# Normalising attention's output straight from PSUM with centred weights, a sort spread over more steps, and later scatters, in an eight-image convolution, scan, attention and expert kernel

## The reference, cut to what matters

```
x = x + ss2d(group_norm(x))      # depthwise conv, scan over 2304 tokens, 256 x 16 states
t = t + attention(ln(t))
t = t + moe(ln(t))               # 8 experts, each token goes to 2 of them

def attention(x):                # linear attention, 8 heads of 16
    q, k, v = split(layer_norm(x, norm_gamma) @ w_qkv.T)
    q = softmax(q, -1) * scale
    k = softmax(k, -2)           # over the tokens
    out = (q @ (k.T @ v)) @ w_out.T
    return (out - mean(out)) * rsqrt(var(out) + 1e-5) * out_gamma
```

## Time and profile before

| | |
|---|---|
| median of three runs | 3913.13 us (3910.83 to 3918.53) |
| the profiled execution: time, span | 3908.72 us, 3906.9 us |
| scans, first to last start | 88 to 3415 us |
| busy: PE, DVE, ACT, POOL | 81%, 76%, 65%, 74% of the span |
| weight loads of PE (beside its matmuls) | 52% |

### The profile page before, as it was taken

One profiled execution on the slowest core, in us unless ns is written; L12 is line 12 of the kernel. 1 busy time (PEld: TensorE's weight loads), 2 busy tenths in 40 slices (PEclk: granted clock), 3 DMA queues, 4 the chain that ended last, 5 costly groups with the idle time before them and its releaser, 6 DMA issues.

```text
span 3906.9 us, 68984 instructions
## 1 busy us (share of the span) xinstructions
PE 3163.4 (81%) x17390; PEld 2012.8 (52%) x17390; DVE 2983.4 (76%) x5234; ACT 2553.7 (65%) x6158; POOL 2909.4 (74%) x3055
## 2 busy tenths in 40 slices
...
GB/s 89 221 146 129 157 124 162 120 161 137 221 177 263 153 211 197 222 221 163 233 178 244 158 208 194 231 212 162 231 185 260 157 202 195 235 150 182 241 233 109
...
## 3 DMA queue, kind: packets, MB, share of 16 engines
...
HBM read 596.93 MB, written 100.07 MB: 178 GB/s over the span
## 4 chain that ended last, share of the span: by engine, by line
PE 24%; POOL 22%; issue 21%; DVE 15%; ACT 11%; DMA 4%; ACTq 2%; SPq 1%; POOLq 1%; DVEq 0%; PEldq 0%
POOL prod L698 10%; DVE state L1582 6%; PE ps_conv L901 5%; PE ps_main L967 4%; DVE ps_x L1569 3%; POOL got L821 3%; PE ps_g L1085 2%; DMA dt_rep<-dt_dram 2%; POOL rows_in L798 2%; PE ps_g L1092 2%; POOL hidden L810 2%; PE ps_y L981 2%; ACT dt_rep L1206 2%; PE ps_h L1073 2%; PE ps_x L915 1%
## 5 line engine op out<-in xcount | busy, mean ns | idle before, releaser
L698 POOL TENSOR_TENSOR prod<-state,c_rep 128x384 f32<-128x384 f32 x1536 | 1532.7, 1007 | 608.5 <-DVE state L1582 588.7
L1582 DVE TENSOR_TENSOR_SCAN state<-dt_rep,carry,ps_x 128x384 f32<-128x384 f32 x1280 | 1285.8, 1005 | 0.0
L1569 DVE TENSOR_TENSOR ps_x<-ps_x,db_rep 128x384 f32<-128x384 f32 x1536 | 852.9, 555 | 243.0 <-PE ps_x L915 223.7
L1206 ACT ACTIVATE dt_rep<-dt_rep,vecs 128x384 f32<-128x384 f32 x1536 | 917.8, 615 | 137.9 <-DMA dt_rep<-dt_dram 77.7
L915 PE MATMUL ps_x<-x_stack,copy 96*128 96x384 bf16 x1536 | 534.2, 350 | 310.8 <-DVE state L1582 306.4
L901 PE MATMUL ps_conv<-gx,w_conv 128*128 128x384 f32 x1728 | 689.6, 507 | 8.0 <-DVE parts L1599 4.6
L915 PEld LDWEIGHTS ps_x<-x_stack,copy 96*128 96x128 bf16 x1536 | 153.9, 100 | 681.6 <-DVE state L1582 493.1
L1390 ACT ACTIVATE g_sb<-ps_g,w_down 128x128 f32<-128x128 f32 x1032 | 304.2, 371 | 231.1 <-PE ps_g L1092 226.3
L901 PEld LDWEIGHTS ps_conv<-gx,w_conv 128*128 128x128 f32 x1728 | 301.1, 195 | 216.6 <-issue 129.6
L1073 PE MATMUL ps_h<-u_t,w_up 128*128 128x128 f32 x2064 | 327.5, 298 | 104.0 <-DVE silu L1799 80.0
L810 POOL TENSOR_TENSOR hidden<-g_sb,silu 128x384 f32<-128x384 f32 x344 | 343.7, 999 | 83.9 <-ACT u_out L1396 74.8
(11 more groups left out here) (256 smaller groups left out, 4958.7 us busy)
## 6 DMA issues: line engine op xcount, KB each, us to landing
dt_rep<-dt_dram SPq DMA_DIRECT2D x384, 768.0 KB
...
dt_dram<-dt SPq DMA_DIRECT2D x192, 96.0 KB
...
```

The costliest lines, as they stand in the source:

```text
L698: pool.tensor_tensor(prod[:, k % HS, :], state[:, k % HS, :], c_rep[:, c % 2, :], ALU.mult).then_inc(s_prod.sem, 1)
L1206: act.activation(dt_rep[:, g % XS, q, :], dt_rep[:, g % XS, q, :], ACT.Exp, scale=decay_rate).then_inc(s_decay.sem, 1)
L1569: dve.tensor_tensor(x_n, x_n, db_rep[:, c % 2, :], ALU.mult).then_inc(s_inflow.sem, 1)
L1582: dve.tensor_tensor_scan(state[:, k % HS, :], dt_rep[:, g % XS, q, :], ps_x[k % XB][:, 0:T], init, ALU.mult, ALU.add).then_inc(s_state.sem, 1)
```

## The change

The output of attention is no longer evacuated, normalised, scaled and added in passes of their own. At the start the weights `w_proj` are centred (their mean over the output channels is taken off, so that the product's mean is zero), and a second copy is multiplied by `out_gamma`. One matmul of 256 columns for a block then gives both the centred output and the scaled one. ACT squares the first half out of PSUM with a running sum, takes logarithm and exponential for 1/rms, and DVE adds the second half times this to `acc`, straight from PSUM. This goes by pairs of blocks (`ap0` to `ap8`, at steps T_AP), with `qT` set between them at T_QT. `acc` now lies in `u_tok`, t1 is read a second time at step 66, and the first read goes to `k_tok`. The sort's steps are spread over 134 to 164, some of its instructions are fused; the first scatter moves from 146 to 168, the second half from 183 to 208 (step 16 of the next pass). Expert tiles, gathers, top-2 and transposes move by some steps.

```diff
-T_XLOAD = 114
+T_XLOAD = 112
-SEQ2 = ("qT0", "qT1", "ao0", "qT2", "ao1", "qT3", "ao2", "qT4", "ao3", "qT5", "ao4", "ao5")
-T_SEQ2 = 68
-T_AGAIN, T_STAT2, T_NORM2, T_STAT3 = 81, 82, 86, 98
-T_GAMMA = tuple(87 + g + g // 2 for g in range(NC))
-T_NORM3 = (102, 103, 105, 107, 110, 112)
-T_UT, T_LOGIT = (105, 105, 110, 110, 115, 117), (115, 122)
-T_TOP = ((119, 0, 9), (126, 9, 14), (127, 14, 18))
-T_PLACE = ((120, 0, 3), (121, 3, 6), (122, 6, 9), (128, 9, 12), (129, 12, 15), (130, 15, 18))
-T_CHOSEN, T_RANK, T_SORT = 132, 135, 136
+T_QT, T_AP = (64, 66, 67, 71, 75, 79), (68, 69, 72, 73, 76, 77, 80, 81, 83)
+NA = NT // 2
+T_AGAIN, T_STAT2 = 66, 88
+T_ACC = (79, 87)
+T_NORM2 = (92, 94, 97, 100, 103, 106)
+T_UT, T_LOGIT = (96, 98, 104, 105, 110, 112), (110, 119)
+T_TOP = ((115, 0, 9), (123, 9, 14), (124, 14, 18))
+T_PLACE = ((116, 0, 3), (117, 3, 6), (118, 6, 9), (125, 9, 12), (126, 12, 15), (127, 15, 18))
+T_CHOSEN, T_RANK = (134, 136), 140
+T_SORT = (143, 146, 149, 152, 154, 156, 158, 161, 164)
-AMONG = (81, 84, 87, 90, 93, 96, 99, 102, 107, 112, 119, 126, 132)
+AMONG = (88, 91, 93, 95, 98, 100, 103, 106, 109, 114, 118, 125, 131)
-T_GATHER = tuple(2 * SC + t for t in (34, 36, 39, 41, 44, 46, 49, 51, 66, 69, 72, 75, 102, 105, 108, 111, 114, 117))
+T_GATHER = tuple(2 * SC + t for t in (34, 36, 39, 41, 44, 46, 49, 51, 66, 69, 72, 75, 86, 90, 94, 98, 102, 106))
-T_SCATTER = tuple(146 + 15 * k // 8 for k in range(NT)) + tuple(183 + 15 * k // 8 for k in range(NT))
-T_SCATTER_LAST = tuple(146 + k for k in range(NT)) + tuple(165 + k for k in range(NT))
-T_HOLD, SOONEST = T_GATHER[0] - 1, 264
-ENDED, SPREAD, RESUMED = 34, T_SCATTER_LAST[0], T_SCATTER_LAST[-1] + 8
+T_SCATTER = tuple(168 + 2 * k for k in range(NT)) + tuple(208 + 15 * k // 8 for k in range(NT))
+T_SCATTER_LAST = tuple(T_SCATTER[0] + k for k in range(NT)) + tuple(T_SCATTER[0] + 19 + k for k in range(NT))
+ENDED, SPREAD, RESUMED = 50, T_SCATTER_LAST[0], T_SCATTER_LAST[-1] + 8
+T_HOLD, SOONEST = T_GATHER[0] - 1, T_W + SC - (RESUMED - 3)
...
-        acc = x_in = q_tok
+        acc, x_in = u_tok, q_tok
...
# POOL
-                    if t == T_GAMMA[g]:
-                        due(pool, s_xn, m, NC + g + 1)
-                        pool.tensor_tensor(k_tok[:, tiles, :], k_tok[:, tiles, :],
-                                           out_gamma[:, :].unsqueeze(1).broadcast_to([P, TT, D]), ALU.mult).then_inc(s_gam.sem, 1)
-                    if t == T_GAMMA[g] + 1:
-                        pool.tensor_tensor(acc[:, tiles, :], acc[:, tiles, :], k_tok[:, tiles, :], ALU.add).then_inc(s_acc.sem, 1)
...
# PE
-                elif kind == "ao":
-                    for k in range(TT):
-                        ins = pe.matmul(o[:, P * k:P * k + P], turned[:, T * g + P * k:T * g + P * k + P], ctx_o[:, :],
-                                        start=True, stop=True)
+                elif kind == "ap":
+                    for k in range(2):
+                        r = P * (2 * g + k)
+                        ins = pe.matmul(o[:, 2 * D * k:2 * D * k + 2 * D], turned[:, r:r + P], ctx_o[:, :], start=True, stop=True)
...
# ACT, one step behind PE
+                elif kind == "ap":
+                    logs()
+                    act.wait_ge(*full(m, name))
+                    tiles = slice(2 * g, 2 * g + 2)
+                    for k in range(2):
+                        t = 2 * g + k
+                        ins = act.activation(k_tok[:, t, :], aux(name, m)[:, 2 * D * k:2 * D * k + D], ACT.Square, accum_out=mv[:, t, 0:1])
+                    ins.then_inc(s_square.sem, 1)
+                    due(act, s_square, m, g + 1)
+                    act.activation(mv[:, tiles, 1], mv[:, tiles, 0], ACT.Ln, bias=eps_ln, scale=1.0 / D).then_inc(s_aln.sem, 1)
+                    due(act, s_aln, m, g + 1)
+                    act.activation(r2[:, tiles], mv[:, tiles, 1], ACT.Exp, scale=-0.5).then_inc(s_rms.sem, 1)
                 elif kind == "ek":
                     if g == 0:
-                        act.wait_ge(*full(m, "xnT5"))
+                        due(act, s_scatter, m, 0)
...
# DVE, two and three steps behind PE
+            def add_rows(m, a):
+                name = f"ap{a}"
+                if a == 0:
+                    due(dve, s_t1in, m, 2)
+                due(dve, s_rms, m, a + 1)
+                for k in range(2):
+                    t = 2 * a + k
+                    ins = dve.scalar_tensor_tensor(out=acc[:, t, :], in0=aux(name, m)[:, 2 * D * k + D:2 * D * k + 2 * D],
+                                                   scalar=r2[:, t:t + 1], in1=acc[:, t, :], op0=ALU.mult, op1=ALU.add)
+                ins.then_inc(frees(name, m), 1)
...
# DVE, the sort
-                    tie(m, dve.tensor_copy(place[:, :, :], where[:, :, :]))
-                    tie(m, dve.tensor_scalar(gw[:, 1, :], gw[:, 0, :], 1.0, None, ALU.add))
-                    tie(m, dve.reciprocal(gw[:, 2, :], gw[:, 1, :]))
+                    tie(m, dve.tensor_scalar(gw[:, 1, :], gw[:, 0, :], 2.0, 2.0, ALU.mult, ALU.add))
-                    tie(m, dve.tensor_scalar(u_weight, gw[:, 2, :], 0.5, None, ALU.mult))
+                    tie(m, dve.reciprocal(u_weight, gw[:, 1, :]))
-                tie(m, dve.tensor_scalar(tally[:, 3, :], counts[:, NE * NT:NE * NT + NE], 1.0 / P, None, ALU.mult))
-                tie(m, dve.tensor_tensor(picked[:, :, :], tally[:, 3, :].unsqueeze(2).broadcast_to([P, NE, NT]),
+                tie(m, dve.scalar_tensor_tensor(out=picked[:, :, :], in0=counts[:, NE * NT:NE * NT + NE].unsqueeze(2).broadcast_to([P, NE, NT]),
-                tie(m, dve.tensor_scalar(tally[:, 3, :], tally[:, 3, :], float(P), None, ALU.mult))
...
# SP
-                    due(sp, s_accout, w.j, 1)
-                    apart()
-                    due(sp, s_xn, w.j, 3 * NC)
+                    sp.wait_ge(*full(w.j, f"qT{NC - 1}"))
-                    due(sp, s_scatter, m, 0)
+                    due(sp, s_sorted, m, 0)
```

More of the change, by code:

```diff
@@ L1502, in _ @@
             dve.tensor_copy(copy[:, :, :].rearrange("p (s b) m -> p s (b m)", s=2), prod[0:32 * PARTS, 0:2, 0:256]).then_inc(s_setup.sem, 1)
+            sums, means = gmv[:, 0:1], gmv[:, 1:2]
+            dve.tensor_reduce(sums, w_proj[:, 0, :], AX.X, ALU.add).then_inc(s_centre.sem, 1)
+            dve.wait_ge(s_centre.sem, 1)
+            dve.tensor_scalar(means, sums, -1.0 / D, None, ALU.mult).then_inc(s_centre.sem, 1)
+            dve.wait_ge(s_centre.sem, 2)
+            dve.tensor_scalar(w_proj[:, 0, :], w_proj[:, 0, :], means, None, ALU.add).then_inc(s_centre.sem, 1)
+            dve.wait_ge(s_centre.sem, 3)
+            dve.tensor_tensor(w_proj[:, 1, :], w_proj[:, 0, :], prod[:, 4, 0:D], ALU.mult).then_inc(s_setup.sem, 1)
             whole, rest = prod[0:PARTS, 2, :], prod[0:PARTS, 3, :]
@@ L1655, in finish, with row_stats @@
                     ins.then_inc(s_t1.sem, 1)
-            def row_stats(m, src, g):
-                for t in range(TT * g, TT * g + TT):
-                    ins = dve.bn_stats(st[:, t, :], src[:, t, :])
-                if g == NC - 1:
+            def add_rows(m, a):
[8 more added lines that the diff above has]
+                ins.then_inc(frees(name, m), 1)
+            def row_stats(m, a):
+                dve.wait_ge(*read(m, f"ap{a}"))
+                for t in (2 * a, 2 * a + 1):
+                    ins = dve.bn_stats(st[:, t, :], acc[:, t, :])
+                if a == NA - 1:
                     ins.then_inc(s_stats.sem, 1)
```

137 lines of the change are left out of this document (66 added, 71 removed).

## The result

The changed kernel takes 4059.3 us in the median of four runs (4046.2 to 4068.4), the kernel before 3913.6 beside it: ratio 1.0368, 95% interval 1.0331 to 1.0406. The forecast was 3872 us, so even the direction was wrong. The profiled execution took 4050.9 us, span 4049.1.

The account below looks back on a forecast made before the run. No engine exceeds 81% of the span, so the bound changes by stretch, with DVE never waiting in steps 128 to 143. Five full passes -17.5, last pass -2, tail -20 sum to -39.5 us off 3913.1: forecast 3872, range 3850 to 3892.

Parts of the forecast that it names:

- POOL falls some 5 us behind ... which just covers it. +0.5: Steps 168 to 63: scatters delay POOL, DVE's 2.5 us maximum at step 51 covers it; +0.5 us, ends 0 and +4.
- -1.5, ends -7 and +4: Steps 88 to 127: POOL's relief covers DVE's 0.8 us wait and loosens the rest; -1.5 us a full pass.
- 9 us saved: Steps 128 to 143: sort work leaves, DVE's 45.3 us become about 33.2, the stretch falls from 47.5 to 38.5 us.
- Strewing buys no cheaper sort: Steps 128 to 167: strewn small sort instructions keep their dear price; lone prices would be some 5 us better.
- 3.5 lost: Steps 144 to 167: incoming sort work uses up DVE's 8.3 us idle time; 53.2 us become 56.7.
- +3, ends -1 and +13: Steps 64 to 87: attention's output by pairs loads DVE, ACT and PE; 48.1 us become 51.
- rival 2: Steps 70 to 85: DVE waits for ACT in each pair, 1.5 us for each of nine; total 3943 us, chance 0.13.
- Out go the tiles at 81, 84 and 87 and with them about 2 us: Steps 64 to 87: three expert tiles leave, taking about 2 us each off PE and ACT.
- -20, ends -8 and -32: Tail after the last scan: shorter attention output saves 19 us, tile moves give -11 + 8; -20 us taken in all.
- -11 + 8: Tail: four extra tiles during attention cost 2 us each; four fewer in the stretch after save 2.8 each.
- -3.5 a full pass: One full pass: sum of the stretches, -5.5 + 3 - 1.5 + 0.5 = -3.5 us; five full passes give -17.5.
- Rival 3: Whole kernel: strewn sort fits the gaps and POOL's 12 us come out; -9 a full pass, tail -30, 3833 us, chance 0.11.

Follow-up runs that it names:

- Experiment 1: The changed kernel with the second half of the scatters at steps 12 to 29 of the next pass instead of 16 to 47: 4086.0 us, ratio 1.0446.
- h2: The kernel before with only the new steps of the thirteen early expert tiles (88 to 131 for 81 to 132): 3948.7 us, ratio 1.0115.
- e6: The changed kernel without the expert tiles at 93, 98 and 103, 33 tiles in 137 to 220 for 30: 4114.4 us, ratio 1.0524.
- e7: The changed kernel with the second half of the logits at 122 for 119, its top-2 and index searches three steps later: 4013.1 us, ratio 1.0245.
- e5: The changed kernel with the last six gathers back at their old steps, 102 to 117 for 86 to 106: 4045.6 us, ratio 1.0336.
- experiment 2: The changed kernel with the sort back at its old steps 132 to 144, fused instructions kept: 4043.3 us, ratio 1.0327.
- experiment 9: The changed kernel with sort, scatters and gathers at old steps, second logits and top-2 later, tile of step 93 at 85: 3982.1 us, ratio 1.0174.
- experiment 10: The kernel before with only the thirteen early expert tiles at their new steps, their weight loads seven steps later: 3948.7 us, ratio 1.0115.
- experiment 8: The changed kernel with sort, scatters and gathers at old steps, second half of logits and top-2 three steps later, tiles unchanged: 3946.1 us, ratio 1.0084.
- e3: The changed kernel with sort and scatters at their old steps, the rest as changed: 3992.9 us, ratio 1.0207.

## Why the prediction was wrong, step by step

**"POOL falls some 5 us behind ... which just covers it. +0.5"** (steps 168 to 63) failed, and it is the clearest miss. That POOL falls behind was right, and so was the chain, the fold ahead of L911 in PE's order. DVE's 2.5 us maximum does lie in the fold's wait of 4.6 us (2774.1 to 2778.7 us; the maximum runs from 2775.0 to 2777.6). But it doesn't cover what comes behind the wait: the fold and the matmuls up to L911 run at the lower clock, DVE stands 4.8 us behind its maximum, and 2.0 more before the next inflow. I had no term for that, and none for the clock. It costs +8.1 a pass, twice the upper end of +4. Experiment 1 shows the cause; it also shows that with the same scatters at 12 to 29 steps 24 to 39 cost 10.7 more.

**"-1.5, ends -7 and +4" for steps 88 to 127** failed: +14.4. I had counted POOL's relief and a sum of PE's work that fits (81 us of 91.4), and no order. Three things broke it, each measured: the tiles' denser steps (h2: +11.2 under the old attention; e6: -8.7 in steps 88 to 111 without three of them), the logits at step 119 behind a gate that isn't ready, with the lower clock behind it in most passes (e7: -7.2), and the gathers from step 86 (e5: some -2 clear of the spread). Together they are more than 14.4, so they overlap or something else was won; the moved statistics, for which ACT waits at step 92, were not tried by themselves. POOL's relief was real (71.5 us busy of 108.0, had 81.7 of 91.4) and bought nothing.

**Steps 128 to 143: "9 us saved".** Right in kind, 5.7 measured: DVE's busy time is 34.05 us where I had 33.2, but the stretch takes 40.6 where I had 38.5 (seventh pass; 41.8 in the mean). Strewing buys no cheaper sort, as I had it: DVE's busy time in 128 to 167 is 86.1 us strewn (34.05 and 52.07) and 86.3 dense (41.21 and 45.12, experiment 2). But strewing is not what saves: at their old steps the fused instructions and the early index searches already give 4.4 of the 5.7 (e2: 43.1).

**Steps 144 to 167: "3.5 lost", out of idle time used up.** Failed: +8.3. The step "the 8.3 us in which it stood idle are used up" is wrong. DVE has as much idle time after as before (10.1 us for 8.3), since it stands at the end of each turn of a loop (scan, gate, tile, spreading matmul, inflow) and not beside it. Net of the two stretches +2.6, where I had -5.5; undoing the strewing (experiment 2) brings -6.0 a pass. I named this as what would make me wrong: if 144 to 167 grows by what 128 to 143 gives.

**Steps 64 to 87: +3, ends -1 and +13.** Right: +2.1. DVE's waits in 2814.2 to 2865.4 us are 3.3 us in all, 2.9 of them for PE; DVE's waits for the exponential are 0.4 us a pass at most in the second to seventh pass, where rival 2 had 13, so it had nothing to it. ACT's squares cost 0.27 and their reads 0.20 us, by these groups of ACT in the stretch:

```profile
L1365 ACT ACTIVATE mv<-mv,vecs 128x2 f32<-128x2 f32 x9 | 2.7, 296 | 0.3
L1362 ACT ACTIVATE big_k<-ps_g 128x128 f32<-128x128 f32 x10 | 2.6, 272 | 2.0 <-PE ps_g L1017 2.0
...
L1362 ACT ACTIVATION_READ_ACCUMULATOR big_k<-ps_g 128x1 f32 x10 | 2.0, 203 | 0.0
...
L1367 ACT ACTIVATE r<-mv 128x2 f32<-128x2 f32 x9 | 1.8, 203 | 0.3
```

That is 1.4 us a pair, where I had 1.8. What I didn't charge is the price of the place: the pairs hold banks that tiles need (experiment 9 shows it for one tile), three tiles left, and their cost falls in the next stretch. I had booked them as "Out go the tiles at 81, 84 and 87 and with them about 2 us", a gain here, and only as PE's 2.1 us there. By experiment 10 that move alone costs more than all that experiment 8 still loses.

**The tail: -20, ends -8 and -32.** Failed: +4.1. Stretches of the tail after: from the first normalisation to the context, to the second normalisation, to the logits' end:

```profile
3598.30:3655.30 57.00, 36.91 (x164) 27.95 (x164) 9.70 (x8) 25.12 (x50) 39.36 (x40) 0.71 0.31 87
3655.30:3693.20 37.90, 25.25 (x130) 20.29 (x129) 11.91 (x41) 26.98 (x92) 19.65 (x27) 0.86 0.53 153
3693.20:3719.40 26.20, 19.96 (x159) 19.11 (x158) 5.26 (x33) 21.09 (x62) 19.05 (x21) 0.93 0.68 208
```

and the same of before, in two (to the context; to the logits' end):

```profile
3464.80:3507.30 42.50, 31.48 (x190) 25.05 (x191) 10.44 (x10) 29.04 (x62) 27.39 (x28) 0.84 0.40 118
3507.30:3575.80 68.50, 43.37 (x278) 40.04 (x278) 14.81 (x72) 43.64 (x117) 54.89 (x71) 0.78 0.51 161
```

From the context to the logits it is 64.1 us for 68.5: the short way through PSUM saves 4.4, not 19. What DVE's sums waited for in the second stretch:

```profile
L1676 DVE SCALAR_TENSOR_TENSOR big_u<-ps_x,r,big_u 128x128 f32<-128x128 f32 x18 | 5.5, 346 | 17.7 <-ACT r L1367 12.3 <-DMA big_u<-t_dram 4.9 <-issue 0.6
```

Here, with no scans, DVE does wait for 1/rms (12.3 us) and 4.9 us for the second read of t1; and ACT loads six tables (L1188, L1183, 1.28 us each) between pairs and tiles, where from the context to the logits' end it loaded four before. Ahead of it 14.5 us are lost, at a clock of 0.71: POOL is busy 39.4 us of the 57.0 where it had 27.4 of 42.5. Eleven scatters (10.9 us) stand in that stretch where none stood, since in the last pass, too, they now come in the steps in which attention starts. That this is their doing was not tried by itself; with the old sort and scatters (e3) the tail is 490.1, 5.8 us shorter. The other term, four more tiles beside the attention and a shorter stretch behind it (-11 + 8), did not come about either: between context and logits' end 8 tiles run where 9 did, and behind them the tail is 1.4 us shorter. The rest of the +4.1 is 4.6 us won ahead of the first normalisation.

**The sum.** Forecast: -3.5 a full pass. Measured: +25.5. Of the forecast's own working only 64 to 87 and the sign of 128 to 143 stood. The upper end of my range left out every case in which a moved piece meets another; the chance of 0.13 for slower was put on a mechanism (waits in the pairs) that came to 0.4 us a pass. Rival 3's 3833 us isn't what its terms give either: five passes at -9 and the tail at -30 make 3838.
